# Leaving out 36 unread TensorE matmuls in the first layer of a four-layer graph network kernel

## The chip, the cores and the metric

The kernel runs on one NeuronCore of a Trainium2 chip. The metric is device time in microseconds for one execution of the whole program. Five engines work beside each other, each through its own list of instructions in order, and wait for one another on semaphores: TensorE (PE, matmuls into PSUM), VectorE (DVE), ScalarE (ACT), GpSimd (POOL) and SyncE (SP, which here issues DMAs).

## What is computed

Four graph layers follow each other on `x` (16 graphs, 512 nodes, 128 features), each with a residual sum and a layer norm. The change is in the first pass, which does layer L0 and the matmul half of L1:

```python
# L0: a diagonal graph convolution, so that every power of adj is a factor for each node
adaptive = softmax(relu(node_vec1 @ node_vec2), axis=1)
outputs = [x]
for adj in (support0, support1, adaptive):
    x1 = x * sum(adj, axis=1)[None, :, None];  outputs.append(x1)
    x1 = x1 * sum(adj, axis=1)[None, :, None]; outputs.append(x1)
x = layernorm(x + concatenate(outputs, axis=2) @ W + b)
# L1: normalised adjacency, then two dense layers, each with a batch norm over all graphs and nodes
A_hat = (A + I) * dinv[:, None] * dinv[None, :]      # dinv = rsqrt(row sums + column sums - diagonal)
agg = einsum('nm,bmd->bnd', A_hat, x)
h = relu(batchnorm(agg @ W1.T + b1));  out = batchnorm(h @ W2.T + b2)
x = layernorm(x + out)
# L2 (two graph layers and LSTMs over windows of nodes) and L3 (8 Euler steps) follow
```

## The kernel before

The program has two halves. `first_half` (line 146) does L0 and L1 for all 16 graphs, `second_half` (line 945) does L2 and L3 in groups of two graphs. Each value that needs full precision is split in a high and a low fp32r part, and a product is three matmuls (`matmul3`, lines 141 to 143: high x high, high x low, low x high).

`phase_a` in `first_half` runs ten slots, q = 0 to 9, and calls on every engine a function `slot(q, now, more, one, two)`. A slot takes the products of pair q of graphs (`now`, q < 8), the aggregation of pair q-1 (`one`) and the hidden layer of pair q-2 (`two`), so three pairs are under way at once. On TensorE a slot is, in this order:

- `products(q, t)` for the node tiles t = 0 to 3: 12 matmuls each, x against the mixed L0 weights, 384 and 256 columns wide. Tile 0 waits for the split x of pair q (`xt_hi` from ScalarE's L444, `xt_lo` from GpSimd's L319); tiles t wait for VectorE to have finished tile t-2 (`mixed`, L684).
- `hidden(q - 2, i)`: 6 matmuls of 512 columns.
- `aggregate(q - 1, i)`: 12 matmuls of 512 columns for each of the two graphs. It waits for the split layer-norm output (`x1_lo`, GpSimd's L330; for the last pair VectorE's L728), and in slot 1 also for the split `A_hat`, block by block (`ahat_lo`, GpSimd's L338).

In slot 0 TensorE also spreads `dinv` over all partitions into PSUM bank 7 (L903, four plain fp32 matmuls with `ones`), which waits for ScalarE's L494 and is read by VectorE's L667.

Slots 0 and 1 hold work that later slots lack: the chain from the adjacency to `A_hat`. In slot 1 ScalarE scales the first term of tile 1 (L487, waits for `products(1, 1)`), then normalises graph 0 (L505), then casts the four blocks of `A_hat` (L531); GpSimd waits for the first of these and then subtracts (L338, L330), adds biases (L325) and splits the next pair's x (L319), all in its own order.

`keep_busy(times, bank)` (line 822) issues `times` matmuls of 512 columns from the weights `wmix_h` into a PSUM bank. Nobody reads what they write, and each next real use of the bank starts with a clearing matmul. There are 64 of them: 12 before L903 and 8 behind it in slot 0, 12 before `aggregate` in slot 1, 4 in slot 8 before the last pair's `aggregate`, 12 before the first batch norm and 16 behind the last `second`. All are line L826:

```python
def keep_busy(times, bank):
    operand = wmix_h[:].rearrange("p k d -> p (k d)")
    for _ in range(times):
        pe.matmul(banks[bank][:], wmix_h[:, 0, :], operand[:, 0:N], start=True, stop=True)
```

Of the kernel before, what the change touches and what calls it, by code (L numbers as in the profile page):

```python
# [31 lines left out]
def need(eng, sem, value):  # L32

    if isinstance(value, int) and value <= 0:
        return
    eng.wait_ge(sem, value)
# [98 lines left out]
PAIRED = B // 2  # L135


def matmul3(pe, dst, lhs, rhs, start, stop, **kw):

    (lh, ll), (rh, rl) = lhs, rhs  # L140
    pe.matmul(dst, lh, rh, start=start, stop=False, **kw)  # L141
    pe.matmul(dst, lh, rl, start=False, stop=False, **kw)  # L142
    return pe.matmul(dst, ll, rh, start=False, stop=stop, **kw)  # L143


def first_half(nc, sem, psum, banks, ident, exponent, scale2, shift2, x_t, adj_n, adj_t, nv1_t, nv2, l0_w, l0_b,
# [6 lines left out]
    with ExitStack() as ctx:  # L153
# [77 lines left out]
        def z_banks(q, i):  # L231

            return banks[6:8] if q < PAIRED - 2 else banks[2 * i:2 * i + 2]
# [19 lines left out]
        def tile(ap, i):  # L253
            return ap[:, i * P:(i + 1) * P]
# [5 lines left out]
        def phase_a(slot):  # L260

            for q in range(PAIRED + 2):
                slot(q, q < PAIRED, q + 1 < PAIRED, 1 <= q <= PAIRED, q >= 2)
# [556 lines left out]
        @block.tensor  # L820
        def _(pe):
# [6 lines that stand above are left out]
            pe.wait_ge(ones_ready, 1)  # L828
            for _ in range(4):
                pe.matmul(tile(banks[0][:], 0), ones[:], ones[:], start=True, stop=True)  # L830
            pe.wait_ge(c_nv, 32)
            for t in range(NT):
                pe.matmul(banks[4 + t][:], tile(nv1s, t), nv2s, start=True, stop=True).then_inc(pe_setup, 1)
            pe.wait_ge(c_w, 48)
            pe.matmul(tile(banks[3][:], 0), ones[0:1, :], bias0[:], start=True, stop=True).then_inc(bias_spread, 1)
            pe.wait_ge(weights_ready, 1)

            def products(q, t):
                if t == 0:
                    pe.wait_ge(xt_hi, 2 * q + 2)  # L840
                    pe.wait_ge(xt_lo, 2 * q + 2)
                need(pe, mixed, NT * q + t - 1)
                first = 3 * (t % 2)
                wh, wl = wmix_h[:].rearrange("p k d -> p (k d)"), wmix_l[:].rearrange("p k d -> p (k d)")
                for i in range(2):
                    x = (tile(xth[:, i, :], t), tile(xtl[:, i, :], t))
                    matmul3(pe, psum[:, first + i, 0:3 * D], x, (wh[:, 2 * D:5 * D], wl[:, 2 * D:5 * D]), True, True)
                    mm = matmul3(pe, psum[:, first + 2, 2 * D * i:2 * D * (i + 1)], x, (wh[:, 0:2 * D], wl[:, 0:2 * D]), True, True)
                mm.then_inc(prod_done, 1)

            def hidden(q, i):
                if q >= PAIRED - 2:
                    pe.wait_ge(agg_lo, 2 * q + i + 1)
                    pe.wait_ge(mixed, NT * PAIRED)
                    pe.wait_ge(z_kept, HT * (2 * (q - 1) + i + 1))
                elif i == 0:
                    pe.wait_ge(agg_lo, 2 * q + 2)
                else:
                    pe.wait_ge(z_kept, HT * (2 * q + 1))
                for h in range(HT):  # L860
                    matmul3(pe, z_banks(q, i)[h][:], (tile(w1h[:], h), tile(w1l[:], h)), (aggh[:, i, :], aggl[:, i, :]),
                            True, True).then_inc(z_done, 1)

            def aggregate(q, i):
                pe.wait_ge(x1_lo, 2 * q + i + 1)
                if q < PAIRED - 1:

                    need(pe, z_kept, HT * 2 * q)
                else:
                    pe.wait_ge(agg_lo, 2 * q - 1 + i)  # L870
                for t in range(NT):
                    if q == 0 and i == 0:
                        pe.wait_ge(ahat_lo, t + 1)
                    mm = matmul3(pe, AGG[i][:], (x1h[:, i, t, :], x1l[:, i, t, :]), (ahat_h[:, t, :], ahat_l[:, t, :]),
                                 t == 0, t == NT - 1)
                mm.then_inc(agg_done, 1)

            def slot(q, now, more, one, two):
                if now:
                    products(q, 0)  # L880
                if q == 0:
                    pe.wait_ge(logits_ready, NT)
                    pe.wait_ge(bias_ready, 1)
                if now:
                    products(q, 1)
                if q == 2:
                    pe.wait_ge(w1_lo, 1)
                if two:
                    hidden(q - 2, 0)
                if now:  # L890
                    products(q, 2)
                if two:
                    hidden(q - 2, 1)
                if q == PAIRED:
                    keep_busy(4, 4)
                if now:
                    products(q, 3)
                if q == 0:

                    keep_busy(12, 7)  # L900
                    pe.wait_ge(dinv_spread, 1)
                    for t in range(NT):
                        mm = pe.matmul(tile(banks[7][:], t), ones[:], diag[:, t, :], start=True, stop=True)  # L903
                    mm.then_inc(pe_setup, 1)
                    keep_busy(8, 6)
                if q == 1:
                    keep_busy(12, 6)
                if one:
                    for i in range(2):
                        aggregate(q - 1, i)  # L910

            phase_a(slot)

            keep_busy(12, 4)

            def second(b, par):
                need(pe, o2_counted, b - 1)
                for h in range(HT):
                    pe.wait_ge(r_ready, HT * b + h + 1)
                    mm = pe.matmul(banks[par][:], w2[:, h, :], act1[:, par, h, :], start=(h == 0), stop=(h == HT - 1))  # L920
                mm.then_inc(o2_done, 1)

            def spread_column(v):
                pe.wait_ge(cols_ready, v + 1)
                for t in range(NT):
                    mm = pe.matmul(tile(banks[2 + v][:], t), ones[:], diags[v][:, t, :], start=True, stop=True)
                mm.then_inc(k_bc, 1)

            pe.wait_ge(z_kept, HT * B)
            pe.wait_ge(z_counted, B)  # L930
            spread_column(0)
            for b in range(B):
                second(b, b % 2)
                if b == 1:
                    spread_column(1)
            keep_busy(16, 4)
# [1203 lines left out]
```

## Time and profile before

| | us |
|---|---|
| median of 3 runs | 929.38 |
| lowest, highest | 929.25, 930.15 |
| the profiled execution, device time | 931.06 |
| its span, first to last instruction | 928.5 |
| TensorE busy in the span | 890.5 (96%) |
| mean granted TensorE clock | 0.994 |

The span is read from the start of the first instruction; times in the views are us from there. The profiled execution's own time is 2.56 us above its span and 1.68 us above the median. The granted clock of TensorE is 1.00 at 2.4 GHz and 0.50 at 1.2 GHz. In the first 15 us the view says 1.00 although the spacing of the matmuls is that of the lower level.

### The profile page before, as it was taken

Reading aid. Unit: us, or ns where it says so; the run is one execution under the profiler, and the core shown is the slowest. Engines: PE = TensorE matmul, PEld = TensorE weight load, DVE = VectorE, ACT = ScalarE, POOL = GpSimd, SP = SyncE. Lnnn points to the kernel's source line nnn. Section 1 sums busy time; section 2 is a strip of 40 time slices with the busy share of each in tenths; the row PEclk is TensorE's granted clock in tenths of the full one; section 3 lists DMA queues with packets and bytes.
Section 4 is the critical chain, followed back from the end, with each engine's and each line's share of the span. In section 5 each row is a group of like instructions: output and inputs, shape, how many; then the busy total and the mean of one; then the engine's idle time right before and its main releaser. Section 6 shows DMA issues by size and latency. Waiting matters only on the chain.

```text
span 928.5 us, 14540 instructions
## 1 busy us (share of the span) xinstructions
PE 890.5 (96%) x4990; PEld 771.5 (83%) x4990; DVE 670.9 (72%) x1588; ACT 564.8 (61%) x1231; POOL 326.4 (35%) x531
## 2 busy tenths in 40 slices
PE   9899999988989999999999999999999999999996
PEld 6788886366778699988989898998989899978986
DVE  6789997775687776677677767767676777665744
ACT  6467675954664775577467647746773775566341
POOL 3856563830121620352144226203421631330121
PEclk9999999999999999999999999999999999999998
DMA  5321211320101101010101200110120001001000
GB/s 186 128 78 58 69 46 46 125 79 25 35 20 39 35 1 58 1 46 23 46 9 39 69 1 14 44 58 1 46 69 1 12 12 47 1 12 35 1 23 23
DMA packets 26594, 38.54 MB, mean 42 GB/s; under 512 B 3333, under 2 KB 12422, under 8 KB 26010
## 3 DMA queue, kind: packets, MB, share of 16 engines
q1 hardware_dynamic: 26088, 36.05, 11.8%
q10 hardware_dynamic: 434, 1.57, 0.5%
q8 instruction: 39, 0.64, 0.3%
q14 instruction: 33, 0.27, 0.1%
HBM read 21.89 MB, written 15.73 MB: 41 GB/s over the span
## 4 chain that ended last, share of the span: by engine, by line
PE 47%; DVE 12%; ACT 8%; POOL 7%; issue 5%; ACTq 0%; DVEq 0%; POOLq 0%
PE psum L141 14%; PE psum L143 13%; PE psum L142 13%; PE psum L1863 2%; PE psum L1864 2%; ACT gate L1438 2%; PE psum L1867 2%; POOL out_rstd L1371 1%; DVE x L1637 1%; DVE x_stats L1615 1%; DVE in_h L1605 1%; POOL node_l L1389 1%; POOL x_rstd L1371 1%; ACT raw L1469 1%; ACT gate L1441 1%
## 5 line engine op out<-in xcount | busy, mean ns | idle before, releaser
L1438 ACT ACTIVATE gate<-psum,gate_bias 128x256 f32<-128x256 f32 (+2 forms) x296 | 143.7, 556 | 61.5 <-PE psum L1867 51.2
L141 PE MATMUL psum<-in_h,wih_h 128*128 128x256 f32 (+2 forms) x312 | 107.4, 344 | 7.3 <-DVE in_l L1609 5.0
L143 PE MATMUL psum<-in_h,wih_l 128*128 128x256 f32 (+2 forms) x312 | 104.3, 334 | 0.0
L142 PE MATMUL psum<-in_l,wih_h 128*128 128x256 f32 (+2 forms) x312 | 103.5, 332 | 0.0
L141 PEld LDWEIGHTS psum<-in_h,wih_h 128*128 128x128 f32 x312 | 59.2, 190 | 19.2 <-DVE in_l L1609 9.1
L1405 POOL TENSOR_TENSOR gate<-in_h,in_l 128x512 f32<-128x512 f32 x14 | 17.9, 1306 | 157.9 <-DVE in_l L1609 157.9
L1441 ACT ACTIVATE gate<-cell 128x512 f32<-128x512 f32 (+2 forms) x80 | 40.3, 503 | 50.8 <-DVE cell L1593 40.0
L1590 DVE TENSOR_TENSOR gate<-gate 128x256 f32<-128x256 f32 (+2 forms) x48 | 24.2, 504 | 60.3 <-ACT gate L1438 60.3
L142 PEld LDWEIGHTS psum<-in_l,wih_h 128*128 128x128 f32 x312 | 59.5, 191 | 5.4 <-issue 0.5
L143 PEld LDWEIGHTS psum<-in_h,wih_l 128*128 128x128 f32 x312 | 59.4, 190 | 4.6
L141 PE MATMUL psum<-e_h,shared 128*128 128x384 f32 x180 | 61.6, 342 | 0.2
L142 PE MATMUL psum<-e_l,shared 128*128 128x384 f32 x180 | 60.7, 337 | 0.0
L143 PE MATMUL psum<-e_h,shared 128*128 128x384 f32 x180 | 60.6, 337 | 0.0
L141 PE MATMUL psum<-shared 128*128 128x512 f32 x140 | 56.4, 403 | 1.6 <-DVE shared L728 0.9
L1863 PE MATMUL psum<-st_h,whh_h 128*128 128x256 f32 (+2 forms) x192 | 56.7, 314 | 1.2 <-DVE st_h L1598 1.2
L1864 PE MATMUL psum<-st_h,whh_l 128*128 128x256 f32 (+2 forms) x192 | 56.5, 312 | 0.0
L1398 POOL TENSOR_TENSOR shared<-raw,shared 128x512 fp32r<-128x512 f32 x14 | 18.2, 1299 | 104.8 <-ACT shared L1506 104.8
L143 PE MATMUL psum<-shared 128*128 128x512 f32 x140 | 54.8, 391 | 0.0
L142 PE MATMUL psum<-shared 128*128 128x512 f32 x140 | 54.6, 390 | 0.0
L1363 POOL TENSOR_TENSOR x_mv<-x_stats 128x4 f32<-128x4 f32 x28 | 9.5, 339 | 125.6 <-DVE x_stats L1615 125.6
L682 DVE SCALAR_TENSOR_TENSOR mix<-psum,coef,mix 128x256 f32<-128x256 f32 x96 | 46.3, 482 | 6.9 <-ACT mix L487 4.6
L141 PE MATMUL psum<-adj_h,node_h 128*128 128x512 f32 x120 | 47.6, 397 | 2.7 <-POOL node_l L1389 2.7
(394 smaller groups left out, 2886.6 us busy)
## 6 DMA issues: line engine op xcount, KB each, us to landing
x_spill<-x SPq DMA_DIRECT2D x30, 256.0 KB, 2.0
xt<-in_x_t_dram SPq DMA_DIRECT2D x16, 256.0 KB, 2.7
raw<-x_spill SPq DMA_DIRECT2D x16, 256.0 KB, 3.0
o_spill<-xt SPq DMA_DIRECT2D x14, 256.0 KB, 2.0
xt<-o_spill SPq DMA_DIRECT2D x14, 256.0 KB, 3.4
x<-x_spill SPq DMA_DIRECT2D x14, 256.0 KB, 3.6
out_dram<-raw SPq DMA_DIRECT2D x14, 256.0 KB, 2.3
raw<-in_adj_t_dram ACTq DMA_DIRECT2D x1, 1024.0 KB, 8.8
```

The source lines that it names most:

```text
L141: pe.matmul(dst, lh, rh, start=start, stop=False, **kw)
L142: pe.matmul(dst, lh, rl, start=False, stop=False, **kw)
L143: return pe.matmul(dst, ll, rh, start=False, stop=stop, **kw)
L682: chain.link(nc.vector.scalar_tensor_tensor(out=m, in0=scaled_block(t, k), scalar=coef[:, k - 1, t:t + 1], in1=m, op0=ALU.mult, op1=ALU.add))
L1371: chain.link(nc.gpsimd.tensor_tensor(rstd, rstd, exponent[:, 0:rstd.shape[-1]], ALU.pow))
L1398: nc.gpsimd.tensor_tensor(low[:], x3[:, j, :, :], f32(high[:]), ALU.subtract).then_inc(x3_lo, 1)
L1438: nc.scalar.activation(gate[q][:, 0:n], banks[GATE_BANK[q]][:, 0:n], ACT.Tanh if q == 2 else ACT.Sigmoid, bias=gate_bias[:, p - 1, q:q + 1 ...
L1441: nc.scalar.activation(gate[2][:, 0:n], cell[:, 0:n], ACT.Tanh).then_inc(tanh_ready, 1)
L1590: nc.vector.tensor_tensor(gate[0][:, 0:n], gate[0][:, 0:n], gate[2][:, 0:n], ALU.mult)
L1863: pe.matmul(bank, tile(whh_h[:, p - 2, :], q), st_h[:, 0:n], start=False, stop=False)
L1864: pe.matmul(bank, tile(whh_l[:, p - 2, :], q), st_h[:, 0:n], start=False, stop=False)
L1867: pe.matmul(banks[GATE_BANK[q]][:, 0:n], tile(whh_h[:, p - 2, :], q), st_l[:, 0:n], start=False, stop=True).then_inc(gate_sum, 1)
```

## The change

The four calls of `keep_busy` inside `phase_a`'s slots are taken out, 12 + 8 + 12 + 4 = 36 matmuls. The 12 before the first batch norm and the 16 after the last `second` stay, and no other line changes (lines behind 907 have numbers lower by 7 in the changed kernel, so L903 becomes L899).

```diff
@@ TensorE's slot(q, now, more, one, two) in first_half @@
                 if two:
                     hidden(q - 2, 1)
-                if q == PAIRED:
-                    keep_busy(4, 4)
                 if now:
                     products(q, 3)
                 if q == 0:
-
-                    keep_busy(12, 7)
                     pe.wait_ge(dinv_spread, 1)
                     for t in range(NT):
                         mm = pe.matmul(tile(banks[7][:], t), ones[:], diag[:, t, :], start=True, stop=True)
                     mm.then_inc(pe_setup, 1)
-                    keep_busy(8, 6)
-                if q == 1:
-                    keep_busy(12, 6)
                 if one:
                     for i in range(2):
                         aggregate(q - 1, i)
```

TensorE's list at the seam of slots 0 and 1, in the kernel before (the last product of slot 0, the unread matmuls, the spread of `dinv`, the first products of slot 1):

```order
51 L143 MATMUL psum<-wmix_h,shared 128x256
52 L826 MATMUL psum<-wmix_h 128x512 x12
53 L903 MATMUL psum<-z,ones 128x128 x4
54 L826 MATMUL psum<-wmix_h 128x512 x8
55 L141 MATMUL psum<-wmix_h,shared 128x384
56 L142 MATMUL psum<-wmix_l,shared 128x384
```

and in the changed kernel:

```order
51 L143 MATMUL psum<-wmix_h,shared 128x256
52 L899 MATMUL psum<-z,ones 128x128 x4
53 L141 MATMUL psum<-wmix_h,shared 128x384
54 L142 MATMUL psum<-wmix_l,shared 128x384
```

Between the products of the two slots only the four matmuls of the spread are left; nothing else changed its place. At the end of slot 1, and in slot 8, the unread matmuls go in the same way and `aggregate` follows the matmul that stood ahead of them.

## Rows read from the trace of the kernel before

**Rows 1.** The page: TensorE's busy time, and its granted clock in 40 slices.

```profile
PE 890.5 (96%) x4990; PEld 771.5 (83%) x4990; DVE 670.9 (72%) x1588; ACT 564.8 (61%) x1231; POOL 326.4 (35%) x531
...
PEclk9999999999999999999999999999999999999998
```

**Rows 2.** Timeline of TensorE, slots 0 to 2: start, us, engine, line, tiles, [idle before].

```profile
11.30 0.69 PE L141 MATMUL psum<-wmix_h,shared 128*128 128x384 f32 x1
...
14.67 0.52 PE L141 MATMUL psum<-wmix_h,shared 128*128 128x384 f32 x1
...
21.45 2.94 PE L826 MATMUL psum<-wmix_h 128*128 128x512 f32 x12
24.24 1.05 PE L903 MATMUL psum<-z,ones 128*128 128x128 f32 x8
25.05 2.09 PE L826 MATMUL psum<-wmix_h 128*128 128x512 f32 x8
27.47 0.41 PE L141 MATMUL psum<-wmix_h,shared 128*128 128x384 f32 x1 [0.33 <-issue]
...
29.31 0.34 PE L141 MATMUL psum<-wmix_h,shared 128*128 128x384 f32 x1
...
34.28 0.44 PE L141 MATMUL psum<-wmix_h,shared 128*128 128x384 f32 x1 [3.06 <-DVE mix L684]
...
38.04 2.95 PE L826 MATMUL psum<-wmix_h 128*128 128x512 f32 x12
40.83 0.39 PE L141 MATMUL psum<-shared 128*128 128x512 f32 x1
...
46.90 0.42 PE L141 MATMUL psum<-wmix_h,shared 128*128 128x384 f32 x1 [0.44 <-issue]
```

**Rows 3.** Timeline of ScalarE in slots 0 and 1.

```profile
22.03 1.27 ACT L494 ACTIVATE z<-ident,dinv 128x128 f32<-128x128 f32 x4
...
31.26 0.47 ACT L487 ACTIVATE mix<-psum,coef 128x256 f32<-128x256 f32 x1 [1.28 <-PE psum L143]
31.72 1.65 ACT L505 ACTIVATE x<-mix,shift,rstd 128x128 f32<-128x128 f32 x4
33.28 2.16 ACT L531 CAST shared<-z 128x512 fp32r<-128x512 f32 x4
```

**Rows 4.** Timeline of GpSimd in slots 0 and 1.

```profile
26.08 1.29 POOL L319 TENSOR_TENSOR shared<-xt,shared 128x512 fp32r<-128x512 f32 x1
...
33.96 2.54 POOL L338 TENSOR_TENSOR shared<-z,shared 128x512 fp32r<-128x512 f32 x2 [3.25 <-ACT shared L531]
...
38.39 1.32 POOL L330 TENSOR_TENSOR shared<-x,shared 128x512 fp32r<-128x512 f32 x1
...
45.47 1.33 POOL L319 TENSOR_TENSOR shared<-xt,shared 128x512 fp32r<-128x512 f32 x1
```

**Rows 5.** Timeline of VectorE in slots 0 to 2.

```profile
28.89 2.72 DVE L667 SCALAR_TENSOR_TENSOR z<-raw,dinv,psum 128x512 f32<-128x512 f32 x4
31.53 0.16 DVE L711 SCALAR_TENSOR_TENSOR shift<-mv,rstd 128x8 f32<-128x8 f32 x1
...
49.91 0.17 DVE L711 SCALAR_TENSOR_TENSOR shift<-mv,rstd 128x8 f32<-128x8 f32 x1 [1.16 <-POOL rstd L110]
```

**Rows 6.** Timeline of TensorE at 306 us and at 828 us.

```profile
306.56 1.99 PE L2075 MATMUL psum<-raw 6*128 6x256 f32 x8 [1.04 <-ACT raw L1560]
...
827.97 0.65 PE L141 MATMUL psum<-in_h,wih_h 128*128 128x340 f32 x1 [2.10 <-DVE in_l L1609]
```

**Rows 7.** Windows: length, busy PE, PEld, DVE, ACT, POOL, then granted clock, DMA.

```profile
309.20:312.40 3.20, 3.00 (x8) 1.82 (x6) 3.17 (x8) 2.38 (x6) 2.85 (x9) 0.50 0.01 3
828.00:831.20 3.20, 3.20 (x11) 3.20 (x12) 1.62 (x3) 2.35 (x6) 1.83 (x5) 0.50 0.28 82
```

**Rows 8.** Timeline of TensorE in slot 8.

```profile
145.87 1.08 PE L826 MATMUL psum<-wmix_h 128*128 128x512 f32 x4
147.85 0.50 PE L141 MATMUL psum<-shared 128*128 128x512 f32 x1 [0.90 <-DVE shared L728]
```

## The prediction, made before the changed kernel ran

> **What bounds the kernel now.** I read the page first: TensorE is busy 96% of the span at a granted clock of full speed in nearly all slices [rows 1]. That says that TensorE's clock matters everywhere, but not that its instructions in slots 0 and 1 do. For those I went through the timelines of the four engines between 11 and 50 us. TensorE has real waits there: 3.06 us before 34.28 for VectorE, and short ones before 27.47 and 46.90 [rows 2]. What it waits for at 27.47 is GpSimd's second split of x, which runs from 26.08 to 27.37 [rows 4]. What it waits for at 46.90 is the same split for the next pair, 45.47 to 46.80; that one stands at the end of a list of GpSimd work that runs from 33.96 without one idle bracket [rows 4]. GpSimd's list in turn began 3.25 us late because it waited for ScalarE's first block of A_hat (L531 at 33.28), which stands behind L505 at 31.72, which stands behind L487 at 31.26, which waited 1.28 us for TensorE's products(1, 1) [rows 3]. So slots 0 and 1 are bounded by a chain TensorE 27.47 to 31.2, ScalarE to 33.9, GpSimd to 46.8, and then TensorE again. VectorE hangs on it too: at 49.91 it has waited 1.16 us for GpSimd [rows 5]. From there VectorE, ScalarE and TensorE feed each other slot by slot, so what is lost before slot 2 I carry to the end in full.
>
> **What the removed matmuls cost by themselves: nothing.** The 36 matmuls take about 0.23 us each (12 from 21.45 to 24.24, 2.79 us) [rows 2].
> - The 12 ahead of L903. ScalarE's L494 starts at 22.03 and lasts 1.27 us, so dinv is ready at 23.30 [rows 3]; L903 starts at 24.24 [rows 2] and could start some 0.9 us sooner. Its reader, VectorE's L667, comes at 28.89, held by VectorE's own list [rows 5]. Gain 0.
> - The 8 behind L903 start at 25.05 and take 1.9 us, to about 26.95 [rows 2], under the wait for GpSimd that ends at 27.37 [rows 4]. Gain 0.
> - The 12 in slot 1, 38.04 to 40.83 [rows 2]. The first aggregate could start when L330 is done, 38.39 + 1.32 = 39.71 [rows 4], so 1.1 us sooner. But the next thing that TensorE must do, products(2, 0), waits until 46.80 for GpSimd, whose list does not depend on aggregate. Gain 0, with 1.1 us as the upper bound.
> - The 4 in slot 8, from 145.87 to about 146.8, lie ahead of an idle 0.90 us that ends with VectorE's L728 at 147.85 [rows 8]. Gain 0.
>
> **What their going does to the clock.** Without them TensorE is idle from 21.45 to 23.3 (1.9 us), works on L903 for 0.8 us, and is idle from 24.1 to 27.4 (3.3 us): 6.0 us with 0.8 us of work, where before the only idle is 0.33 us [rows 2]. Does the clock survive that? The trace shows three things. It was at full speed after the 3.06 us of idle before 34.28: the next tile's pace is the fast one, since the unread matmuls at 38.04 again take 0.23 us each [rows 2]. It fell at 828, where TensorE had been idle for 2.10 us and at work before [rows 6], and stood at 0.50, which is 1.2 GHz, through all 3.2 us of the window from 828.00 [rows 7]. It fell at 309 after 1.04 us of idle and 2 us of matmuls that use 6 rows of the array [rows 6], again for at least 3.2 us [rows 7]. So 2 to 3 us of idle amid full work is already enough at one place and not at the next; it depends on when it comes. Two such idles with only 0.8 us between them are emptier than either place at which it fell. I take it that the clock falls before 27.47.
>
> By the Trainium skill, TensorE: Matmul & The Clock Gate, section HAM oscillation, the clock is taken back only for an idle gap of a length that neither of the two idles here quite reaches; by that rule the time would stay at 929.4. The row at 827.97, where 2.10 us were enough, speaks against it, and I go by the row.
>
> **What a low clock costs there.** A tile of products, 12 matmuls, takes 14.67 - 11.30 = 3.37 us at the lower level at the start of the kernel and 29.31 - 27.47 = 1.84 us at the upper [rows 2]. The chain needs two tiles from 27.47, products(1, 0) and (1, 1). Both slow: 2 x 1.53 = 3.06 us later. If instead the clock is back after 3.2 us of slow work, as it was at 309 and 828 [rows 7], half of that is lost, 1.6 us. If the slow time is partly spent in the idle before 27.47, less than 1 us is lost; below zero I see nothing, as no engine gets faster. Nearest to this place are the two dips, and the start of the slow stretch can lie on either side of 27.47. I take 2.2 us, between 1.6 and 3.1. Slack against it: ScalarE's L505 also waits for VectorE's L711, 31.53 + 0.16 = 31.69, against its start at 31.72 [rows 3, 5], so the slack is 0.03 us and the delay goes through to L531, GpSimd and products(2, 0) at 46.90.
>
> What was covered and is bare now: the idle before aggregate in slot 1. TensorE ends products(1, 3) at 38.04 [rows 2], and with GpSimd 2.2 us late L330 ends at 41.9, so TensorE idles 3.9 us there. If the clock falls again, it meets two aggregates of 12 matmuls at 0.23 us. At full speed and back to back from 41.9 they end at 47.4, against products(2, 0) at 49.1, a slack of 1.7 us; a dip of 3.2 us costs 1.6. The second aggregate has a wait of its own for GpSimd, which eats into that slack, so the cost is 0 to 0.6 us, and I take 0. In slot 8 idle grows from 0.90 us to 1.8 us in a place where TensorE is waited for; a dip right behind 147.85 costs 3.2 / 2 = 1.6 us. I take 0 as the likelier.
>
> **The sum.** 0 - 0 + 2.2 + 0 = +2.2 us. Against the profiled execution's span of 928.5 that gives 930.7, with its time 931.06 + 2.2 = 933.3; that execution stands 1.7 us above the median, so on the median 929.38 + 2.2 = **931.6 us**, 0.24% slower.
>
> **Rivals.**
> - The clock comes back inside the two tiles, because it fell early and some of the slow stretch passes while TensorE has nothing to do: +0.9 us, 930.3. For it: TensorE works from 23.3 to 24.1, and the fall could come as early as 24 us. Against: in both dips shown TensorE worked all through the slow window [rows 7].
> - The clock holds at 27.47: 929.4, no change. For it: the 3.06 us before 34.28 did no harm. Against: 828. The deciding point is whether the 0.8 us of L903 count for enough.
> - A second dip besides the first, in slot 8 or in slot 1's aggregate: +2.2 + 1.5 = +3.7, 933.1. For it: both places lose their cover, and ScalarE waits for TensorE's aggregate in slot 8.
> - The other side: the clock holds and slot 1's aggregate, 1.1 us sooner, is what the end hangs on: 928.3. It decides from the point where GpSimd's split would be done before TensorE, which is at 46.80 against 46.3; it is not, so this is the least likely. It would still lie within 0.2%.
>
> **How the numbers follow.** Forecast 50%, clock back early 20%, clock holds 12%, second dip 13%, gain carried 5%. The range leaves out most of the last and the tip of the fourth: 929.2 to 933.4. Differences below 0.2% (1.9 us: 927.5 to 931.2) can't be told from no change. Slower by more: all of the second-dip case and the forecast where it costs more than 1.9 us, 43 of its 50: 56%. Faster by more: 3%, for what I don't see. The rest, 41%, is within 0.2%.
>
> **What would show it.** In the changed trace: granted clock 0.50 in some stretch between 24 and 33 us, and a tile from 27.47 taking over 2.5 us instead of 1.84. L487 for tile 1 at 33.4 instead of 31.26, GpSimd's first L338 at 36.2 instead of 33.96, its last L319 at 47.7 instead of 45.47, products(2, 0) at 49.1 instead of 46.90, and the last product chain of slot 7 the same 2.2 us later. If L338 still starts at 33.96, the clock held and the forecast is wrong. If L338 is late and slot 8 is not, the delay was taken up by slack that I don't see. If the end moves by more than slot 2 does, a later dip is in it.

## The result

| | before | changed |
|---|---|---|
| median, 6 executions each | 929.97 us | 933.65 us |
| lowest to highest | 929.25 to 930.15 | 931.74 to 934.32 |
| ratio, 95% interval | | 1.0034, 1.0023 to 1.0045 |
| profiled span | 928.5 | 932.1 |
| mean granted clock | 0.994 | 0.986 |

The changed kernel is 0.34% slower, 2.1 to 4.2 us by the interval; the two medians differ by 3.68 us. The median of 933.65 lies 2.05 us above the forecast 931.6 and 0.25 us above the top of the range, 933.4. The range stood on a base of 929.38; the ratio on that base gives 932.5, which is inside it. A second comparison with 11 executions of the changed kernel (below, `after_again`) gave 1.0026, 1.0013 to 1.0038.

The page of the changed kernel: TensorE's busy time, and its granted clock in 40 slices of 23.3 us (answers to [rows 1]).

```profile
PE 888.3 (95%) x4954; PEld 770.0 (83%) x4954; DVE 670.9 (72%) x1588; ACT 565.0 (61%) x1231; POOL 325.9 (35%) x531
...
PEclk9799999999999999999999999999999999999998
```

TensorE has 36 matmuls fewer and is busy 2.2 us less, though 36 of 0.23 us are 8.3 us: the rest ran longer. The slice with the 7 is the second, 23 to 47 us. The lower clock is not a matter of one execution: all 17 executions of the changed kernel had a mean granted clock of 0.991 or less, while the 28 of the kernel before that ran beside the last 11 of them had 0.991 or more, 19 of them 0.994.

TensorE's timeline in slots 0 to 2 of the changed kernel (answers to [rows 2]); L899 is the former L903:

```profile
23.36 1.16 PE L899 MATMUL psum<-z,ones 128*128 128x128 f32 x8 [1.73 <-ACT z L494]
27.45 0.66 PE L141 MATMUL psum<-wmix_h,shared 128*128 128x384 f32 x1 [2.94 <-issue]
...
30.79 0.52 PE L141 MATMUL psum<-wmix_h,shared 128*128 128x384 f32 x1
...
34.26 0.44 PE L141 MATMUL psum<-wmix_h,shared 128*128 128x384 f32 x1 [0.60 <-DVE mix L684]
...
42.01 0.51 PE L141 MATMUL psum<-shared 128*128 128x512 f32 x1 [3.75 <-POOL shared L330]
...
49.21 0.34 PE L141 MATMUL psum<-wmix_h,shared 128*128 128x384 f32 x1
```

The idle before 27.45 ends when it did before. But the first tile (products(1, 0), 12 matmuls) now takes 30.79 - 27.45 = 3.34 us instead of 1.84. ScalarE's L487 behind the second tile, and GpSimd's list behind that (answers to [rows 3, 4]):

```profile
33.70 0.47 ACT L487 ACTIVATE mix<-psum,coef 128x256 f32<-128x256 f32 x1 [2.19 <-PE psum L143]
34.07 1.64 ACT L505 ACTIVATE x<-mix,shift,rstd 128x128 f32<-128x128 f32 x4
35.61 0.60 ACT L531 CAST shared<-z 128x512 fp32r<-128x512 f32 x1
```

```profile
36.29 2.53 POOL L338 TENSOR_TENSOR shared<-z,shared 128x512 fp32r<-128x512 f32 x2 [5.61 <-ACT shared L531]
...
40.69 1.26 POOL L330 TENSOR_TENSOR shared<-x,shared 128x512 fp32r<-128x512 f32 x1
...
47.72 1.29 POOL L319 TENSOR_TENSOR shared<-xt,shared 128x512 fp32r<-128x512 f32 x1
```

L338 starts 36.29 - 33.96 = 2.33 us late, the last L319 47.72 - 45.47 = 2.25, and products(2, 0) 49.21 - 46.90 = 2.31. The delay goes through the chain nearly without loss, as its 0.03 us of slack [rows 3, 5] let expect. The granted clock in four windows of the changed kernel (columns as in [rows 7]; it stands third from the end):

```profile
26.10:32.80 6.70, 5.35 (x20) 5.38 (x21) 6.50 (x17) 0.47 (x1) 3.92 (x4) 0.50 0.31 82
43.20:46.50 3.30, 3.30 (x10) 2.52 (x9) 2.24 (x6) 0.00 (x0) 3.30 (x4) 0.50 0.94 392
145.00:155.00 10.00, 7.79 (x34) 5.78 (x33) 7.40 (x17) 5.76 (x12) 5.09 (x6) 1.00 0.29 105
227.50:230.80 3.30, 3.30 (x8) 2.65 (x9) 1.18 (x2) 1.77 (x3) 0.00 (x0) 0.50 0.00 0
```

The clock was at 1.2 GHz from 26.1 to 32.8, over nearly all of the two tiles; again from 43.2, behind 3.75 us of idle; and from 227.5, where before had none. Such a time at 1.2 GHz is called a low stretch below. In slot 8 the clock held, and the step there is still 2.2 us (answer to [rows 8]):

```profile
150.08 0.50 PE L141 MATMUL psum<-shared 128*128 128x512 f32 x1 [1.82 <-DVE shared L728]
```

Laid side by side matmul by matmul, the two traces are 2.2 us apart from 49 to 225 us, 3.5 to 3.7 from 231 on, and 3.6 us at the end. So the profiled loss is two steps: 2.3 us before products(1, 1) is done, of which 2.2 stay, and 1.35 us at 227 us. The low stretch at 43 adds nothing: products(2, 0) is as late as GpSimd.

### The profile page after: what moved, and what is told of

It reads as the page before. It is cut to its first block, busy times and chain, and to the rows that moved or that the text cites. A ratio compares the mean times of both kernels' runs of the same rounds, so it can differ in the third digit from the quotient of the medians.

```text
span 932.1 us, 14468 instructions
## 1 busy us (share of the span) xinstructions
PE 888.3 (95%) x4954; PEld 770.0 (83%) x4954; DVE 670.9 (72%) x1588; ACT 565.0 (61%) x1231; POOL 325.9 (35%) x531
## 4 chain that ended last, share of the span: by engine, by line
PE 48%; DVE 11%; ACT 8%; POOL 7%; issue 4%; ACTq 0%; DVEq 0%; POOLq 0%
PE psum L141 14%; PE psum L143 13%; PE psum L142 13%; PE psum L1860 2%; PE psum L1856 2%; PE psum L1857 2%; ACT gate L1431 2%; POOL out_rstd L1364 1%; POOL node_l L1382 1%; POOL x_rstd L1364 1%; DVE x L1630 1%; ACT raw L1462 1%; DVE x_stats L1608 1%; DVE in_h L1598 1%; ACT raw L1525 1%
## 5 line engine op out<-in xcount | busy, mean ns | idle before, releaser
L1434 ACT ACTIVATE gate<-cell 128x512 f32<-128x512 f32 (+2 forms) x80 | 40.2, 503 | 50.7 <-DVE cell L1586 39.9
L141 PE MATMUL psum<-shared 128*128 128x512 f32 x140 | 57.0, 407 | 6.3 <-POOL shared L330 3.8
L143 PE MATMUL psum<-shared 128*128 128x512 f32 x140 | 55.5, 397 | 0.0
L142 PE MATMUL psum<-shared 128*128 128x512 f32 x140 | 55.3, 395 | 0.0
```

What stands on the lines that cost most here:

```text
L1434: nc.scalar.activation(gate[2][:, 0:n], cell[:, 0:n], ACT.Tanh).then_inc(tanh_ready, 1)
```

## The experiments

The theory: the matmuls taken out cost nothing themselves, but they kept TensorE's clock up, and the loss is what the chain behind it loses while the clock is low. The rivals: a lost microsecond comes from the delay's effects later on and not from the clock, or from the other places that lost their cover. (Unread matmuls that run under a wait are its cover; an idle without them is bare.) Single executions of one kernel spread over 2 to 7 us (one of the kernel before at 3069.56 us aside), so 8 to 12 of them fix a ratio to within some 0.8 to 1.5 us, and the profiles, one execution each, show the mechanism. Every diff is against the kernel before, if nothing else is said.

**Slot 0's 20 alone.**

```diff
-                    keep_busy(12, 7)
-                    keep_busy(8, 6)
```

> Only the 20 unread matmuls of slot 0 are out; the 12 of slot 1 and the 4 of slot 8 stay. My theory (the clock falls in the bare stretch from 21.45 to 27.45, and all of the loss up to slot 8 is from there): GpSimd's first L338 at 36.3 instead of 33.96, products(2, 0) near 49.2, the whole within 0.5 us of the changed kernel, +3.2 to +3.7 us on before. Rival (the dip that the changed kernel has at 43 us, or slot 8's bare idle, carries a part): +1 to +2 us less than the changed kernel.

Measured: ratio 1.0036 (1.0023 to 1.0049), median 933.21 us against 930.13. TensorE:

```profile
27.86 0.66 PE L141 MATMUL psum<-wmix_h,shared 128*128 128x384 f32 x1 [2.93 <-issue]
...
49.66 0.41 PE L141 MATMUL psum<-wmix_h,shared 128*128 128x384 f32 x1 [0.90 <-issue]
```

GpSimd's L338 starts at 36.76. products(2, 0) is 2.76 us late, of which 0.39 us stand already before 27.86: the start of this execution was that much slower. The later trace has the same step, 1.33 us, at 228 us. Slot 0 alone makes a loss as large as the whole change's.

**The other 16 alone.**

```diff
-                if q == PAIRED:
-                    keep_busy(4, 4)
-                if q == 1:
-                    keep_busy(12, 6)
```

> Only the 12 unread matmuls of slot 1 and the 4 of slot 8 are out; the 20 of slot 0 stay. My theory: within 0.5 us of before; slot 1's aggregate starts at 39.7 instead of 40.83 and products(2, 0) still at 46.9. Rival (aggregate sooner carries to the end): -1.1 us. Second rival (the clock falls in slot 8's bare idle of 1.8 us): +1.6 us, with a granted clock of 0.5 somewhere from 145 to 152 us.

Measured: 1.0018 (1.0006 to 1.0031), 931.51 us. My theory expected no loss here, and that was wrong. Its profile doesn't show the loss: the clock was low from 34.3 to 41.1 us, but products(2, 0) starts at 47.59, 0.69 us late, of which 0.75 stood before slot 1, and the 1.82 us of idle in slot 8 (ending at 148.55) did not lower the clock. The two parts were run apart, below, to tell which place it is.

**The delay without the low clock.**

```diff
-                    keep_busy(8, 6)
+                    keep_busy(20, 6)
```

> The kernel before with 20 instead of 8 unread matmuls behind L903, so that products(1, 0) starts near 29.8 instead of 27.47 while TensorE never rests: the delay of the changed kernel without its low clock in slots 0 and 1. If the changed kernel's third loss, the dip at 227 us (1.3 us), comes from all later work standing 2.3 us later: +3.2 to +3.7 us, with a dip near 227 us. If that dip is the fallen clock's doing, or chance: +2.0 to +2.5 us and no dip at 227.

Measured: 1.0032 (1.0022 to 1.0042), 933.09 us. The mean granted clocks of its ten executions, 0.992 to 0.996, are those of the kernel before (0.991 to 0.996). TensorE:

```profile
25.07 4.82 PE L826 MATMUL psum<-wmix_h 128*128 128x512 f32 x20
29.73 0.34 PE L141 MATMUL psum<-wmix_h,shared 128*128 128x384 f32 x1
...
31.48 0.34 PE L141 MATMUL psum<-wmix_h,shared 128*128 128x384 f32 x1
...
48.93 0.41 PE L141 MATMUL psum<-wmix_h,shared 128*128 128x384 f32 x1 [0.89 <-issue]
```

The first tile starts at 29.73 and takes 1.75 us, at full clock; L338 starts at 36.03 and products(2, 0) at 48.93, 2.0 us late. So 2 us of delay at this place cost 2.3 us at the end of this profile and 3 us by the medians, whatever makes them: the clock is the cause of the delay in the changed kernel, and the chain does the rest. The median lies between the two outcomes that were expected.

This profile has no low stretch at 227 us. The matmul behind the idle there, first in this run and then in the changed kernel:

```profile
227.27 0.50 PE L141 MATMUL psum<-in_h,wih_h 128*128 128x512 f32 x1 [1.08 <-DVE in_l L1734]
```

```profile
227.39 0.79 PE L141 MATMUL psum<-in_h,wih_h 128*128 128x512 f32 x1 [1.07 <-DVE in_l L1727]
```

The idle is the same, 0.12 us apart. Over all 14 profiles, the four in which this matmul starts at 227.39 or later have a low stretch right behind it, and the ten in which it starts at 227.27 or sooner have none. That fits a step that comes once the work is late enough, but no experiment moved this place alone; what decides it stays open.

**One of slot 0's two idles covered.** Against the changed kernel, the 8 behind L903 back:

```diff
                     mm.then_inc(pe_setup, 1)
+                    keep_busy(8, 6)
```

> The changed kernel with the 8 unread matmuls behind L903 put back, so that the 1.9 us of idle ahead of L903 stays bare and the one behind it shrinks from 3.0 to about 1.4 us. If one of the two idles must be covered and no more: the time of before within 0.5 us, a tile from 27.45 in 1.84 us. If each bare idle is enough to lower the clock: +2 to +3.7 us.

Measured: 1.0020 (1.0011 to 1.0029), 931.40 us, the same as with the 16 of slots 1 and 8 out and slot 0 whole. TensorE:

```profile
23.21 1.16 PE L900 MATMUL psum<-z,ones 128*128 128x128 f32 x8 [1.73 <-ACT z L494]
24.12 2.09 PE L826 MATMUL psum<-wmix_h 128*128 128x512 f32 x8
27.31 0.41 PE L141 MATMUL psum<-wmix_h,shared 128*128 128x384 f32 x1 [1.10 <-issue]
...
29.15 0.33 PE L141 MATMUL psum<-wmix_h,shared 128*128 128x384 f32 x1
```

A tile takes 29.15 - 27.31 = 1.84 us. By the medians the 8 behind L903 give back all that slot 0's 20 gave, and the 1.73 us of idle ahead of L900 (the former L903) did not lower the clock. It fell later, in the 3.06 us idle of slot 1, as in `slots_1_8_gone`, and products(2, 0) at 46.67 is not late:

```profile
33.30:40.00 6.70, 5.88 (x21) 5.88 (x22) 4.18 (x10) 5.03 (x11) 6.20 (x6) 0.50 0.36 110
```

The other way round, the 12 ahead back:

```diff
                 if q == 0:
+                    keep_busy(12, 7)
                     pe.wait_ge(dinv_spread, 1)
```

> The changed kernel with the 12 unread matmuls ahead of L903 put back and nothing else, so that the idle behind L903 (about 2.4 us, 25.05 to 27.45) is the bare one. If one covered idle is enough whichever it is: as the kernel with only the 8 behind put back, +1.0 to +1.5 us (the share of slots 1 and 8). If the idle right ahead of products(1, 0) is the one that counts: +2.3 to +3.7 us in most executions.

Measured: 1.0034 (1.0019 to 1.0049), 933.03 us. Its profiled execution kept the clock at 27.50 behind 2.18 us of idle, and was 928.5 us long; the 12 timed ones lie between 930.19 and 936.68. The medians say that the later cover is the one that counts, but the intervals of the two kernels overlap, and no profile caught the fall.

**Slot 8's 4 alone, twice.**

```diff
-                if q == PAIRED:
-                    keep_busy(4, 4)
```

> The kernel before without the 4 unread matmuls of slot 8 alone. If slot 8's bare idle (1.8 us ahead of 147.85) lowers the clock in some executions: those are 1.5 to 2 us slower at a mean granted clock lower by about 0.004, the median +0.7 to +1.5 us, and the slot-8 share of the loss of the kernel without the 16 matmuls of slots 1 and 8 is here. If slot 8 is harmless: within 0.5 us of before.

> The kernel before without the 4 unread matmuls of slot 8, once more, because +2.8 us for it and +1.4 us for the kernel without these 4 and slot 1's 12 do not fit well. If slot 8's share is that of the second: +0.7 to +1.6 us. If that of the first: +2.3 to +3.2 us. A profile with a low stretch near 149 us shows it as a step of 1.6 us at that place, one without shows no step there.

Measured: 1.0034 (1.0022 to 1.0045), 932.90 us, and 1.0031 (1.0014 to 1.0047), 933.60 us. In both profiles the clock falls right behind 1.82 us of idle. The first of them, TensorE and a window:

```profile
148.73 0.50 PE L141 MATMUL psum<-shared 128*128 128x512 f32 x1 [1.82 <-DVE shared L728]
...
149.82 0.63 PE L141 MATMUL psum<-shared 128*128 128x512 f32 x1
...
151.10 0.63 PE L141 MATMUL psum<-shared 128*128 128x512 f32 x1
...
152.38 0.50 PE L141 MATMUL psum<-shared 128*128 128x512 f32 x1
```

```profile
149.20:152.60 3.40, 3.40 (x10) 2.62 (x9) 1.28 (x3) 1.22 (x3) 1.64 (x3) 0.50 0.36 152
```

Three matmuls take 1.28 us instead of 0.69; against before the trace moves from 0.88 us late at 148.7 to 2.49 at 152.4. Four unread matmuls of 0.9 us in all, which ran under a wait, are worth 1.6 us at their own place in such an execution. Before, the same place had 0.90 us of idle [rows 8]. That is only half of the 3 us. Both profiles have the low stretch at 227 us too, worth 1.35 us, so that each loses 2.9 us between 147 and 231 us. From the second of them:

```profile
227.80:231.10 3.30, 3.30 (x8) 2.62 (x9) 1.23 (x2) 1.72 (x3) 0.00 (x0) 0.50 0.00 0
```

**Slot 1's 12 alone.**

```diff
-                if q == 1:
-                    keep_busy(12, 6)
```

> The kernel before without the 12 unread matmuls of slot 1 alone. If the idle ahead of slot 1's aggregate costs nothing while the clock is high: within 0.5 us of before. If it carries the loss of the kernel without the 16: +0.7 to +1.5 us, with a low granted clock somewhere in 38 to 47 us and products(2, 0) later than 46.9.

Measured: 1.0018 (1.0005 to 1.0031), 931.19 us, with executions from 928.53 to 935.41. Its profiled execution, 926.7 us, shows nothing lost, although the clock was low over products(1, 2) and (1, 3):

```profile
39.47 0.50 PE L141 MATMUL psum<-shared 128*128 128x512 f32 x1
46.58 0.42 PE L141 MATMUL psum<-wmix_h,shared 128*128 128x384 f32 x1 [0.86 <-issue]
```

```profile
35.20:38.50 3.30, 3.30 (x14) 3.30 (x14) 1.44 (x4) 2.93 (x7) 3.30 (x4) 0.50 0.12 43
```

The next experiment says more on these 12.

**Only 12 of the 36 kept.**

```diff
-                    keep_busy(12, 7)
-                if q == 1:
-                    keep_busy(12, 6)
```

> Only the 8 behind L903 and the 4 of slot 8 stay, 24 unread matmuls are out (the 12 ahead of L903 and the 12 of slot 1). If those two places carry the whole loss: within 0.7 us of before. If slot 1's 12 or the 12 ahead of L903 carry a part: +1 to +2 us.

Measured: 0.9998 (0.9986 to 1.0010), 930.08 us against 930.32: no difference. 24 of the 36 can go. (That the kernel without slot 1's 12 alone came out at 1.0018, with an interval just clear of 1, does not fit this well, and stays open.) For slot 1's 12 the profiles show why they aren't a gain. Both executions here had the clock low over products(1, 2) and (1, 3); it fell within the 3.06 us idle that the kernel before has too. First `slot8_gone_again`, in which slot 1 keeps its 12, then this kernel:

```profile
34.14 0.69 PE L141 MATMUL psum<-wmix_h,shared 128*128 128x384 f32 x1 [3.06 <-DVE mix L684]
...
40.41 2.90 PE L826 MATMUL psum<-wmix_h 128*128 128x512 f32 x12
43.15 0.39 PE L141 MATMUL psum<-shared 128*128 128x512 f32 x1
...
48.61 0.34 PE L141 MATMUL psum<-wmix_h,shared 128*128 128x384 f32 x1
```

```profile
33.30:40.00 6.70, 5.86 (x21) 5.86 (x22) 4.18 (x10) 5.05 (x11) 6.19 (x6) 0.50 0.37 113
```

```profile
33.98 0.69 PE L141 MATMUL psum<-wmix_h,shared 128*128 128x384 f32 x1 [3.06 <-DVE mix L684]
...
40.19 0.40 PE L141 MATMUL psum<-shared 128*128 128x512 f32 x1
...
46.52 0.41 PE L141 MATMUL psum<-wmix_h,shared 128*128 128x384 f32 x1 [0.73 <-issue]
```

```profile
33.00:39.70 6.70, 5.71 (x21) 5.72 (x22) 4.18 (x10) 5.19 (x12) 6.05 (x6) 0.50 0.37 113
```

The products end at 40.4 in one and 40.2 in the other, 2.2 to 2.4 us later than before. With the 12 behind them aggregate starts at 43.15 and products(2, 0) at 48.61, 1.7 us late; without them at 40.19 and 46.52, and nothing is lost. The 12 themselves run at full speed, 43.15 - 40.41 = 2.74 us; they are on the path because the products ahead of them are late. Of what `slot8_gone_again` lost in slot 1 about 1.1 us is left at 69 us and stays: where TensorE alone is late and GpSimd is not, part is made up.

**The changed kernel again**, with no edit.

> The changed kernel once more, for the size of its loss and a second profile. The theory (one low stretch before products(1, 0), then by execution others in slot 1, slot 8 and at 227 us): +3 to +3.7 us, low clock from 24 to 28 us on. If the loss of the first runs was largely chance: +2 us or less.

Measured: 1.0026 (1.0013 to 1.0038), 932.01 us against 930.32. In windows and timeline the same picture before slot 2:

```profile
27.08 0.66 PE L141 MATMUL psum<-wmix_h,shared 128*128 128x384 f32 x1 [2.94 <-issue]
...
48.54 0.34 PE L141 MATMUL psum<-wmix_h,shared 128*128 128x384 f32 x1
```

```profile
25.10:31.80 6.70, 4.72 (x17) 4.75 (x18) 6.16 (x17) 0.47 (x1) 4.55 (x4) 0.50 0.26 82
42.20:45.40 3.20, 3.20 (x9) 2.53 (x8) 2.29 (x7) 0.00 (x0) 3.20 (x4) 0.50 1.00 412
227.50:230.80 3.30, 3.30 (x16) 2.62 (x15) 1.56 (x3) 3.20 (x6) 0.00 (x0) 1.00 0.00 0
```

products(2, 0) is 1.64 us late (2.03 us, if its earlier start at 27.08 is counted), and at 227 us the clock holds. This execution's span is 930.2, 1.7 us above before: one step, and not two.

**More cover than before.** The kernel before with 6 unread matmuls ahead of L2075, and 8 and 7 before the first cells of the last group's third and fourth LSTM:

```diff
+                    if g == G - 1 and t == 0 and p > 2:
+                        need(pe, gate_on, evicted(g, c, 0))
+                        for _ in range(8 if p == 3 else 7):
+                            pe.matmul(banks[GATE_BANK[0]][:], tile(wih_h[:, 0, :], 0), wih_h[:, 0, :], start=True, stop=True)
                     pe.wait_ge(state_ready, CELLS * g + first)
...
-                pe.wait_ge(vt_kept, 1)
                 pe.wait_ge(bc_kept, 1)
+                for _ in range(6):
+                    pe.matmul(UB[1][:], tile(wih_h[:, 0, :], 0), wih_h[:, 0, :], start=True, stop=True)
+                pe.wait_ge(vt_kept, 1)
```

> The kernel before with unread matmuls at three more idles, which it has at 305.5 (6 of them, ahead of L2075), 825.9 (8) and 848.0 us (7). If idles cost there through the clock: fewer low stretches, none at 828, the median 1 to 3 us below before. If they are harmless or the added matmuls only delay: within 0.5 us, or up to 1 us slower.

Measured: 0.9993 (0.9980 to 1.0006), 929.10 us against 930.14. The low stretch at 828 us is gone and the one at 309 is not:

```profile
309.40:312.70 3.30, 3.12 (x8) 1.95 (x7) 3.27 (x9) 2.18 (x6) 2.91 (x10) 0.50 0.01 2
825.00:832.00 7.00, 6.66 (x35) 5.69 (x34) 4.95 (x10) 6.29 (x15) 5.71 (x12) 1.00 0.13 37
```

From 828 to 832 us this trace gains 1.5 us on before. But four profiles of other runs without this cover (`late_but_warm`, `only_8_behind`, `slot1_gone`, `eight_and_four`) have no low stretch at 828 either, so that it is not shown that the added matmuls took it away. The matmuls ahead of L2075 (now L2080) did not help and moved it by 0.3 us. And with two places more (5 before the first cell, 5 before the first gather of the second pair):

```diff
+                    if (g, c) == (0, 0):
+                        pe.wait_ge(pre0_ready, 1)
+                        for _ in range(5):
+                            pe.matmul(banks[GATE_BANK[0]][:], tile(wih_h[:, 0, :], 0), wih_h[:, 0, :], start=True, stop=True)
                     pe.wait_ge(h_ready, GB * g + j + 1)
...
+                    if n == 2:
+                        pe.wait_ge(x2_summed, n + 1)
+                        for _ in range(5):
+                            pe.matmul(FB[j][:], tile(wih_h[:, 0, :], 0), wih_h[:, 0, :], start=True, stop=True)
                     pe.wait_ge(x2_lo, n + 1)
```

> The kernel with unread matmuls at three more places, and 5 each at two others that it has: before the first LSTM cell (223.9 us) and before the first gather of the second pair (277.0 us). If every idle over about a microsecond next to others costs by the clock: -1.5 to -2.5 us on before and fewer low stretches. If the first three took all that is to be had: -1 us, as there.

Measured: 0.9996 (0.9987 to 1.0006), 930.04 us. The mean granted clock of its profile is 0.995 and the median did not move: neither kernel beats the one before by what can be measured.

## Why the prediction was right, and where it was not

- **Nothing gained by leaving out the matmuls themselves: right.** L899 came 0.88 us sooner and nobody used it; the wait before 27.45 ended where it did; `eight_and_four` takes 24 of them out at no change.
- **The clock falls before 27.47: right.** In all three profiles of a kernel with slot 0 bare it fell between 25.0 and 26.6 us and stayed at 1.2 GHz over most of both tiles. One of the rows that I weighed was luck of one execution: the 3.06 us of idle before 34.28, which did no harm in the profile of before, has a low stretch in or shortly behind it in eight of the nine other profiles that have this idle. By the rule of the Trainium skill (TensorE: Matmul & The Clock Gate, HAM oscillation) neither idle was long enough and the time would have stayed. That did not hold: the two idles measured 1.73 and 2.94 us and the clock fell, as it did behind 1.82 us of idle (slot 8) and 2.10 us [rows 6].
- **The term of 2.2 us: right in size, and partly by luck.** It was 2.33 us at L338 in one profile and 1.6 to 2.0 us at products(2, 0) in another. But 2.2 was a value between two priced cases, one dip of 3.2 us (1.6) and both tiles slow throughout (3.06). What came, in the profile of the changed kernel, was one low stretch of 6.8 us, twice a dip of [rows 7], that began 1.4 us before the tiles did and ended within the second. That the delay would pass nearly undiminished through ScalarE and GpSimd is what the rows show, and `late_but_warm` shows it without the clock.
- **The second idle in slot 1, 0 to 0.6 us, taken as 0: right.** TensorE idled 3.75 us (3.9 said), the clock fell at 43.2, and products(2, 0) did not feel it. What I did not see is that before's 12 matmuls there cost time, about 1.1 us at the end, in an execution whose clock fell at 33 us; with 24 of the 36 out, these 12 among them, nothing was lost.
- **Slot 8, taken as 0: mis-sized.** The mechanism and its price of 1.6 us stood there, with 13% for a second low stretch in slot 8 or slot 1; the term was put at 0 as the likelier without a reason. In both profiles with slot 8 alone bare the clock fell, at the price of 1.6 us; the rest of the 3 us by the medians (1.3 to 4.4 over the two intervals) is the stretch at 227 us in both. In the changed kernel itself slot 8's term was 0 in both profiles.
- **What was carried to the end: too little in one of two profiles.** The 2.2 us became 3.6 by a low stretch at 227 us, a place that the prediction does not name. The size is that of the rival with a second dip (+3.7, 933.1), but not the place. The trace of before had there idles of 0.7 and 1.1 us that did no harm in its one execution. I priced the places that the change lays bare, and not those that it moves.
- **The base.** The median of before was 929.38 over 3 executions and is 930.1 to 930.3 over larger sets; 0.6 us of the difference between 931.6 and 933.65 lie there.

Three things stay open. The shares don't add up: slot 0 alone 1.0036, slot 8 alone 1.0031 to 1.0034, and both with slot 1 1.0026 to 1.0034. The profiles say where to look. Seven of them have slot 8 bare, each with the same 1.8 us of idle. The clock fell behind it in the two of `slot8_gone`, in which slot 1's 12 matmuls stay and the idle ended at 148.73 and 148.84; it held in the five without these 12, in which it ended between 147.61 and 148.55 or at 149.44 and later. Three of the five had slot 0 at full clock, so a low stretch in slot 0 is not what spares slot 8. Whether the moment decides or something else was not tried. Second, what decides the step at 227 us. And third, the intervals are as wide as half the effect, so that the split between 12 ahead and 8 behind rests on medians.

## What to carry to other kernels

A matmul that nobody reads can be worth more than its own time where TensorE would otherwise rest right before work that a long chain waits for. Look for the places where two idles lie close together, as in slot 0; there the later one was, by the medians, the one to cover. Cover is a risk where it can outlast the wait that it hides under: once the work ahead of it is late, as in slot 1 behind a low stretch, the cover itself is on the path. When a change moves later work by some microseconds, idles that did no harm before can lower the clock, and one profile of before doesn't list them.

## What the runs showed of the hardware

Whether an idle lowers the clock is a matter of the execution, and not of its length alone. The 3.06 us idle of slot 1 left the clock at full speed in the profile of before and stood with 0.50 over 6.7 us in three others shown above; the 1.8 us of slot 8 did no harm in the changed kernel and halved the clock in `slot8_gone`; 1.07 us of idle at 227 us halved it in the changed kernel, and 1.08 us at the same place did not in `late_but_warm`. A low stretch on the path costs 1.3 to 1.6 us where it lasts 3.3 us, and nothing where another engine is what the next step waits for (slot 1, 35 to 40 us).

Executions of one kernel differ by 2 to 7 us with nothing changed, for instance 927.84 to 932.36 us over 29 executions of before, where three gave 929.25 to 930.15. The low stretches are a part of that. Another part stands before them: the first tile of slot 1, at 27.47 us in before, starts between 26.35 and 28.26 in the seven profiles whose instructions are the same up to there.
